# Two graph layers on one core: neighbour rows of layer 0 gathered in natural order, one closing block per 128 nodes

## What is computed

```python
h = relu(layernorm(x))
agg = segment_sum(h[src], dst, 6250)
deg = segment_sum(1, dst, 6250)
z = agg / max(deg, 1)[:, None] @ W_l.T + b_l + h @ W_r.T
r = relu(z)
x = x + (r - mean(r)) * rsqrt(var(r) + 1e-5) * gamma + beta
# layer 1: attention (Q, K, V of relu(layernorm(x))) over the same src, dst
```

## Time and profile before

| what | us |
|---|---|
| median of three runs | 3741.74 (3740.89 to 3746.67) |
| profiled execution, whole | 3740.36 |
| profiled execution, span from first to last instruction | 3738.0 |
| busy in the span: PE, DVE, POOL, ACT | 3025.4, 2503.8, 1991.4, 1632.8 |
| mean granted TensorE clock | 0.862 of full speed |

### The profile page before, as it was taken

One profiled execution on the slowest core, in us unless ns is written; L12 is line 12 of the kernel. 1 busy time (PEld: TensorE's weight loads), 2 busy tenths in 40 slices (PEclk: granted clock), 3 DMA queues, 4 the chain that ended last, 5 costly groups with the idle time before them and its releaser, 6 DMA issues. The chain is left out here.

```text
span 3738.0 us, 59649 instructions
## 1 busy us (share of the span) xinstructions
PE 3025.4 (81%) x11648; PEld 1516.3 (41%) x11649; DVE 2503.8 (67%) x4615; ACT 1632.8 (44%) x6216; POOL 1991.4 (53%) x1929
## 2 busy tenths in 40 slices
PE   4776777777777776599998999999999999999640
PEld 2332222222222222488884444444444444444210
DVE  4444333333333333555557999999999999999999
ACT  2331000000000000222226999999999999999410
POOL 1004777777777776111115555555555555555455
PEclk9887766667776767799998999999999999999865
DMA  2334666666666665344446888887888888888337
GB/s 71 110 109 133 176 176 175 177 175 180 176 175 174 176 175 153 113 143 151 147 145 245 276 277 277 278 275 270 274 276 276 276 276 277 277 276 277 104 116 218
DMA packets 263476, 750.48 MB, mean 201 GB/s; under 512 B 54179, under 2 KB 54181, under 8 KB 263402
## 3 DMA queue, kind: packets, MB, share of 16 engines
q0 software_dynamic: 197504, 615.66, 52.1%
q1 hardware_dynamic: 58910, 121.60, 10.1%
q10 hardware_dynamic: 7020, 12.80, 0.9%
HBM read 750.45 MB, written 77.83 MB: 222 GB/s over the span
## 5 line engine op out<-in xcount | busy, mean ns | idle before, releaser
L1080 POOL DMA_INDIRECT kv<-kv_d,src_t x880 | 876.9, 997 | 633.4 <-PE psw L1226 464.1
L831 POOL DMA_INDIRECT rows<-y_d,src_t x880 | 898.0, 1020 | 555.8 <-DVE rows L838 288.1
L1102 ACT ACTIVATE kv<-kv,wgt 128x64 f32<-128x64 f32 x4400 | 1096.8, 334 | 0.0
L1223 PE MATMUL psa<-kv,hot 128*128 128x512 f32 x1760 | 863.6, 613 | 29.1 <-ACT kv L1102 27.7
L921 PE MATMUL pss<-rows,hot 128*128 128x512 f16 x1760 | 632.5, 494 | 273.4 <-DMA rows<-y_d,src_t 238.0
L1132 DVE TENSOR_TENSOR kv<-kv,ps_q 128x1024 f32<-128x1024 f32 x440 | 533.0, 1211 | 32.6 <-PE ps_q L1207 24.0
L1145 DVE TENSOR_REDUCE score<-kv 128x16 f32<-128x1024 f32 x440 | 531.2, 1207 | 0.0
L1019 ACT ACTIVATE var<-var 128x512 f32<-128x512 f32 x2 | 1.3, 629 | 1187.7 <-DVE var L1006 1187.7
L1223 PEld LDWEIGHTS psa<-kv,hot 128*128 128x128 f32 x1760 | 304.1, 190 | 395.9 <-issue 387.1
L1207 PE MATMUL ps_q<-sums,hotT 128*128 x1760 | 454.4, 381 | 0.1
L855 DVE TENSOR_SCALAR rd<-psc 128x1 f32 (+1 forms) x49 | 7.7, 158 | 599.7 <-PE psc L923 599.7
(11 more groups left out here) (191 smaller groups left out, 3620.1 us busy)
## 6 DMA issues: line engine op xcount, KB each, us to landing
kv_d<-o_sb SPq DMA_DIRECT2D x49, 512.0 KB, 2.8
rows<-y_d,src_t POOLq DMA_INDIRECT x880, 3.7
kv<-kv_d,src_t POOLq DMA_INDIRECT x880, 5.3
y_d<-y SPq DMA_DIRECT2D x49, 256.0 KB, 2.0
x_d<-x_sb SPq DMA_DIRECT2D x49, 256.0 KB, 3.2
h_d<-h SPq DMA_DIRECT2D x49, 256.0 KB, 3.4
h1b<-h_d SPq DMA_DIRECT2D x49, 256.0 KB, 2.7
x1b<-x_d SPq DMA_DIRECT2D x49, 256.0 KB, 4.0
```

The costliest lines, as they stand in the source:

```text
L831: pool.indirect_dma_start(rows[:, u, g, :], None, y_d[0:N, :], bass.IndirectOffsetOnAxis(src_t[:, m:m + 1], 0), bounds_check=limit, oob_is ...
L1080: pool.indirect_dma_start(kv[:, u, g, :], None, kv_d[0:N, :], bass.IndirectOffsetOnAxis(src_t[:, m:m + 1], 0), bounds_check=limit, oob_is_ ...
L1102: last = nc.scalar.mul(v, v, wgt[:, u, g * HEADS + h:g * HEADS + h + 1])
L1223: nc.tensor.matmul(pss[:, ds(par, D)], hot[:, u, g, :].bitcast(F32), kv[:, u, g, D:2 * D], start=False, stop=(g == G - 1), skip_group_chec ...
```

## The change

1. `embed` no longer uses PE. DVE and ACT split h, not transposed, into its fp16 parts, which are stored to HBM (`h0_d`) and kept in `sums`. x has three buffers instead of two.
2. The weight preparation moves into `prepare`, between the issue of its index gathers and their use. New tables are built there, among them `nat_t`: src in natural order, 782 columns of 128, read back from `src_pad` by 7 DMAs and transposed.
3. `aggregate` gathers rows of h (the same 2 KB per row) in natural order: 391 groups, 782 gathers, no bounds check. A step finds its group's ring slot in a table; a straddling group stays in its slot for both of its steps. Rows outside a step's window are multiplied by zeros of the one-hot.
4. SP stands between: it waits for a group's landing, tells PE (`ready`), reads from a table (`last_t`) the last step that uses the group four back, waits for it and tells GpSimd (`free`).
5. PE reads four values per step in one load and takes one branch. At a new window w a block does `multiply(w-3)` (24 products: own h by W_r, average by W_l), `turn(w-2)` (8 small matmuls that transpose the fp16 parts of h, 4 transposes of the average) and the zeroing. Both of the first are behind branches of their own.
6. ACT joins aggregate: it scales the sum by 1/degree and makes the high parts. DVE makes the degree, the low parts and a shorter flush, and does so three one-hots ahead of the window's first step instead of one.
7. Eight memsets of the ring go.

The diff, cut to its core:

```diff
-    y_d = nc.dram_tensor("y_d", (WINDOWS * P, 2 * D), F16).ap()
+    h0_d = nc.dram_tensor("h0_d", (WINDOWS * P, 2 * D), F16).ap()
```

In `prepare`, DVE, behind the index columns:

```diff
+                        nc.vector.tensor_scalar(before_g[:, :], step[:, 0:GROUPS], 1.0, cnt[:, 0:1], ALU.add, ALU.is_ge).then_inc(ended, 1)
+                        for k in range(3):
+                            then(nc.vector.tensor_scalar(back_t[k][:, :], win[:, :], -(k + 1.0), 0.0, ALU.add, ALU.max))
+                            then(nc.vector.scalar_tensor_tensor(past_t[k][:, :], win[:, :], k + 1.0, new_t[:, :], ALU.is_ge, ALU.mult))
...
+                        for c in range(NCH):
+                            n = min(P, GROUPS * G - c * P)
+                            dve.wait_ge(turned, 2 * TCH + c + 1)
+                            nc.vector.tensor_copy(nat_t[:, c * P:c * P + n], ps_t[c % 2][:, 0:n]).then_inc(stored, 1)
```

In `embed`, DVE:

```diff
+                        def low(w, b):
                             dve.wait_ge(high, w + 1)
+                            nc.vector.tensor_tensor(slot(w, 1), h[:, b % 2, :], slot(w, 0), ALU.subtract).then_inc(split, 1)
```

In `aggregate`, GpSimd:

```diff
+                        for n in range(GROUPS):
+                            if n >= U:
+                                pool.wait_ge(free, n - U + 1)
                             for g in range(G):
+                                pool.indirect_dma_start(at_ring(n % U, g), None, h0_d[0:N, :],
+                                                        bass.IndirectOffsetOnAxis(nat_t[:, n * G + g:n * G + g + 1], 0)).then_inc(rows_in[n % U], 16)
```

SP:

```diff
+                        def pass_on(n, i, u, release=True):
+                            sp.wait_ge(rows_in[u], 16 * G * (i + 1))
+                            sp.sem_inc(ready, 1)
+                            if release:
+                                last = sp.value_load(last_t[0:1, ds(n - LAG, 1)], min_val=1, max_val=U + STEPS)
+                                sp.wait_ge(ps_made, last)
+                                sp.sem_inc(free, 1)
```

ACT:

```diff
+                        def high_parts(w):
+                            act.wait_ge(turned, w + 1)
+                            act.wait_ge(products, w + 1)
+                            nc.scalar.copy(mT[:, 0, :], ps_m0[:, :])
+                            nc.scalar.copy(hT[:, 0, :], ps_h0[:, :]).then_inc(high, 1)
...
+                        def average(w, par):
+                            act.wait_ge(rd_ready, w + 1)
+                            nc.scalar.mul(mean[:, :], pss[:, par * D:(par + 1) * D], rd[:, 0:1]).then_inc(averaged, 1)
```

DVE:

```diff
+                        def low_parts(w):
+                            dve.wait_ge(high, w + 1)
+                            nc.vector.tensor_tensor(mT[:, 1, :], ps_m0[:, :], mT[:, 0, :], ALU.subtract)
+                            nc.vector.tensor_tensor(hT[:, 1, :], ps_h0[:, :], hT[:, 0, :], ALU.subtract).then_inc(low, 1)
...
+                        def close_before(s):
+                            [new] = load_values(mybir.EngineType.DVE, past_t[0], s, 1, 1)
                             with dve.If(new):
...
                                 dve.wait_ge(ps_made, s + U)
                                 alone(dve)
+                                degree(w, par)
+                                [second] = load_values(mybir.EngineType.DVE, past_t[1], s, 1, 1)
+                                with dve.If(second):
+                                    low_parts(dve.value_load(back_t[1][0:1, ds(s, 1)], min_val=0, max_val=WINDOWS - 1))
+                                [third] = load_values(mybir.EngineType.DVE, past_t[2], s, 1, 1)
+                                with dve.If(third):
+                                    flush(dve.value_load(back_t[2][0:1, ds(s, 1)], min_val=0, max_val=WINDOWS - 1))
```

PE:

```diff
+                        def turn(w):
+                            pe.wait_ge(averaged, w + 3)
+                            pe.wait_ge(low, w + 1)
+                            for c in range(KC):
+                                for part in range(2):
+                                    nc.tensor.matmul(ps_h0[:, c * P:(c + 1) * P], slots[:, ds(w * 2 * WIDTH + part * D + c * P, P)], ident16[:, :],
+                                                     start=(part == 0), stop=(part == 1))
+                            for c in range(KC):
+                                last = nc.tensor.transpose(ps_m0[:, c * P:(c + 1) * P], mean[:, c * P:(c + 1) * P], ident[:, :])
+                            last.then_inc(turned, 1)
...
+                        def multiply(w):
+                            pe.wait_ge(low, w + 2)
+                            pe.wait_ge(taken, w + 1)
+                            for k, (given, weights) in enumerate(((hT, w_r16), (mT, w_l16))):
+                                for c in range(KC):
+                                    for part, of in ((0, 0), (0, 1), (1, 0)):
+                                        last = nc.tensor.matmul(ps_z[:, :], given[:, part, c * P:(c + 1) * P], weights[:, of, c, :],
+                                                                start=(k == c == part == of == 0), stop=(k == 1 and c == KC - 1 and part == 1))
+                            last.then_inc(products, 1)
...
+                                par, new, need, ring = load_values(mybir.EngineType.PE, use_t, s * 4, 4, (U - 1) * G * 2 * D)
...
+                                pe.wait_ge(ready, need)
...
+                        multiply(WINDOWS - 3)
+                        turn(WINDOWS - 2)
+                        multiply(WINDOWS - 2)
+                        turn(WINDOWS - 1)
+                        multiply(WINDOWS - 1)
```

More of the change, by code:

```diff
@@ L797, in aggregate, with windows @@
-        def aggregate(w_r16, bias, S1, S2):
+                            act.wait_ge(h_made, w + 1)
+                            nc.scalar.copy(slot(w, 0), h[:, b % 2, :]).then_inc(high, 1)
+                        def windows(q, buf, after=NB):
+                            for b in range(NB):
+                                rectify(NB * q + b, q, buf, b)
+                                if b == NB - 2:
+                                    deviation(q + 1, after)
+                        deviation(0, NB)
@@ L800, in aggregate @@
+                        for q in range(XB):
+                            windows(q, q)
+                        with act.Fori(1, FOURS // XB - 1) as i:
+                            for k in range(XB):
+                                windows(XB * i + k, k)
+                        for k in range(XB):
+                            windows(FOURS - XB + k, k, NB if k < XB - 1 else 1)
+                        rectify(WINDOWS - 1, FOURS, 0, 0)
+        def aggregate(w_l16, w_r16, bias, S1, S2):
             with ExitStack() as ctx:
-                rows = sb(ctx, "rows", [P, U, G, 2 * D], F16)
+                rows = sb(ctx, "rows", [P, U * G * 2 * D], F16)
```

485 lines of the change are left out of this document (234 added, 251 removed).

## The result

| | before | after |
|---|---|---|
| median of the runs, us | 3742.22 (3740.89 to 3746.67, 4 runs) | 4018.19 (4016.59 to 4019.79, 4 runs) |
| span of the profiled execution | 3738.0 | 4017.2 |
| first gather of aggregate starts | 316.8 | 184.0 |
| last gather starts | 1481.8 | 1708.7 |
| aggregate's last VectorE pass ends | 1490.5 | 1771.4 |

The ratio is 1.073, 95% interval 1.072 to 1.075, where 3486 us, 0.932, had been forecast. By the table: the stages before the gathers gave 132.8 us, the stretch of the gathers took 359.7 more (1524.7 instead of 1165.0), its tail 54.0 more (62.7 instead of 8.7), the rest 1.7 less; the sum is 279.2, which is the difference of the spans.

The account below looks back on a forecast made before the run. Aggregate was taken as paced by GpSimd's number of gathers. 3740.36 - 130 (embed) - 169 (gathers) + 15 (closing block) + 28 (tail) = 3484, given as 3486 us with the median's 1.4 us offset; range 3445 to 3610.

Parts of the forecast that it names:

- Embed and prepare: Stages before the gathers: weight block ends at 70 us, first gather at 187 instead of 316.8, minus 130 us.
- (d): Rival: embed's loop is held by its transfers, 12 us a quad, whole 3531 us; chance 0.10.
- Gathers: Aggregate: 782 gathers at 1.275 us replace 880 at 1.325, GpSimd setting the pace; minus 169 us (145 to 189).
- four prepared steps at 0.92: Aggregate's window chain: TensorE fills VectorE's 6.5 us with opening zeros and these steps, 4.7 us, and stalls 1.8.
- VectorE's load and branch per step fit: Aggregate: they fit into VectorE's 0.38 us gap between one-hots, part of pricing the hand-over and loads at zero.
- chain of 19.0 us per window: Aggregate, one window's last step to the next's: 1.4 us under GpSimd's 20.4 us pace; 21.6 with slow first products.
- The block: Aggregate's window closing: 24 products, 8 small matmuls, 4 transposes fit under GpSimd's pace; plus 15 us, bounds 0 and 59.
- lateness removes such stretches: Closing block: half-clock first products (1.2 us over pace per window) need prior idleness, which being late removes.
- The tail: Last gather's start to aggregate's end: 37 us instead of 8.9, plus 28 us.
- (b): Rival: aggregate is paced by bytes, not gathers; its 1166 us stays, whole 3640 us; chance 0.04.
- (a): Rival: TensorE and VectorE take turns setting aggregate's pace, 23 us per window, whole 3601 us; chance 0.20.
- (c): Rival: TensorE's clock stays at 0.50 through aggregate, 31 us per window, whole 3993 us; chance 0.03.

Follow-up runs that it names:

- e9: e5 with VectorE's aggregate loop cut from eight steps per turn to four; 3632.9 us, ratio 0.971.
- e17: e9 with natural order, TensorE looping over 391 groups at fixed places, turning before multiplying, one packed word per group for VectorE and TensorE; 3523.0 us, ratio 0.942.
- e5: Kernel after with 880 bounds-checked gathers in step order, fixed places, no SyncE hand-over, two one-value TensorE loads; 3664.0 us, ratio 0.980.
- e8: Kernel after without the closing block's 12 products of the mean with W_l; 3868.5 us, ratio 1.035.
- e13: e7 with TensorE waiting through SyncE for a count against a loaded value; 4026.0 us, ratio 1.076.
- e2: Kernel after with VectorE's aggregate loop cut from eight steps per turn to four; 4015.8 us, ratio 1.073.
- e4: Kernel before with TensorE reading its two values out of one four-value load; 3747.5 us, ratio 1.001.
- e1: Kernel after with TensorE loading one packed word per step instead of four values; 4102.1 us, ratio 1.096.
- e7: e6 with the four wide products taking the ring's place from a loaded value instead of a fixed address; 3885.5 us, ratio 1.040.
- e6: e5 with TensorE reading its values by one load of four, two of them unused; 3731.7 us, ratio 1.000.

## Why the prediction was wrong

**Embed and prepare: right.** First gather at 184.0, forecast 187. The tables' last copy ended near 70, as said, and VectorE waited for x once, 5.6 us, as the loop was entered, and a quad took 8.3 to 8.7 us. Rival (d) is out. The stage gave 132.8 us, forecast 130.

**Gathers: the duration was right, the pace was not GpSimd's.** 972 ns mean and 946 median, that of a gather without bounds check. But 566 us of waiting came on top. In e9, where nothing holds GpSimd, the pace is 1.327 a gather, and in e17 (1041 - 72 of waiting) / 781 = 1.24. The term was sound and hidden behind another bound. (Its lower end, 145, does not follow from 1.32 a gather: 1166 - 1032 is 134, which the + 35 in the range has right.)

**The step that failed: "four prepared steps at 0.92" and "VectorE's load and branch per step fit".** The chain of 19.0 us per window took TensorE's step from 848.51 to 849.43. That is the pitch of steps that the sequencer had queued while 12 products ran, here the first three behind an opening (848.51, 849.43, 850.34; the next starts at 851.86). The kernel before has two to four of them behind an opening, and else mostly waits for rows, so that the earlier trace rows and GpSimd's pace hid what a step costs the sequencer. Even that kernel's own step costs 1.6 us when nothing else holds it up: e5 has the same two loads, branch, fixed places and waits, and its "issue" steps are 1.61 apart. I priced SP's hand-over and the table loads for SP, VectorE and the opening, and for TensorE's step, which by the change "reads four values per step in one load", nothing at all. Measured: the load of four 0.988 us (0.29 a step more than two single loads), four dynamic places 0.38, the wait against a loaded value 0.29, together the way from 1.61 to 2.57; the step 2.57 in place of 0.92 for those on the chain, and in place of nothing for the rest, which the forecast had under GpSimd's 20.4. Eight of them are 20.6 us, the whole of GpSimd's window, before any block.

**The block: mis-sized.** 1.1 + 5.3 + 1.5 and 0.5 of zeros were foreseen, 8.4. Measured from the end of the step ahead (811.8) to the first product of the next (822.97) are 11.2: the gap is 1.69 and the first dozen ran at 1.2 GHz, 5.30 instead of 2.7. This block is one of the longer ones; over 45 the mean is 10.5, with a first dozen of 4.76. That is 2.1 us x 48 = 101 us, and e8 shows that nearly all of the block counts. The prediction had the slow first half in its upper bound and set it aside because "lateness removes such stretches" of idleness. It doesn't where TensorE is late because of its own sequencer: the engine then pauses in every step, and comes into the block at the low clock. With cheaper steps the first dozen's mean is 3.5 us in e5, 3.4 in e9 and, with the turning ahead of it, 2.8 in e17.

**The tail.** 62.7 us, forecast 37. The 30 us between the last step and the coefficients came as said (1740.5 to 1771.4). The other 32 are the last gather to the last step: eight groups lay in the ring, because TensorE was behind, where I had counted one.

Sum: 3486 - 3 for the start, + 513 for the stretch of the gathers (1524.7 where 1012 was forecast), + 26 for the tail is 4022; 4018 was measured.

**The rivals.** (b) is out: e17 moves 196 GB/s in this stage, above the 174 of before, so bytes did not pace it. The "small, variable" that the Trainium skill, DMA: Bandwidth & Descriptors, section "Anatomy of one DMA", gives for descriptor generation is contradicted by e9 against e17: the same bytes, 98 gathers fewer and each without the bounds check (946 ns against 998), 125 us. (a) named the right sign of trouble, GpSimd's gaps naming SP, and the wrong size, 23 us a window against 32.1; and what stood against it, that an engine that falls behind stays busy and at the high clock, did not hold: TensorE was behind and busy 72% of the time, at a mean clock of 0.67. (c) came out at 3993 and looks like a hit at 4018. It is not: its mechanism was products at 1.2 GHz in all steps, and the pitch is 2.57 at either level (826.81 and 807.30 above), so the right time was luck. The low clock came with TensorE pausing for its sequencer: from e5 to e13 only loads, addresses and a wait were added, and the granted clock from 184 to 1340 us fell from 0.87 to 0.68. Only the first dozen of a block pays for it. My chance of 0.04 for slower rested on never having asked what a step costs when nobody else holds it up.

## What to carry to other kernels

Before moving work to where an engine "has slack", price the step of each engine as if all others were free: loads by value (0.25 to 0.29 us each here, together or apart), register operations, dynamic addresses and register waits by some 0.1 to 0.3 us, and compare the sum with the pace that will be left. A pitch that stays the same while the named releaser and the clock change is a sequencer's. And an edit that is worth nothing (the short loop in e2, the four-value load in e4) may be worth 30 to 70 us once the bound above it is gone, so retry small edits after each large one.

## What the runs showed of the hardware

- A sequencer's load of four values lasts 988 ns against 287 for one: 234 for each further value and some 50 fixed.
- A register operation recorded with 32 to 46 ns takes about 0.1 us of a queue's time (an estimate from e1, eight in 0.83 us, and from e7 against e6, three in 0.38 us).
- A semaphore wait against a loaded value, with the register work of its bounds, cost 0.29 us a step more than a wait against the loop's own count (e13 against e7), also in steps that did not have to wait.
- A compare-and-branch in TensorE's queue lasted 207 ns in the median, 75 at the least (440 in the kernel after). The Trainium skill, Advanced Engine Details and Errata, section "Control Flow Timing", gives about 108 ns; the measurement decides here.
- Steps with two single loads, a branch and fixed addresses follow each other 1.61 us apart when nothing else holds them up (e5); steps that the sequencer had queued behind other work, 0.92 apart, with the same matmuls (kernel before).
- VectorE's loop of 8 steps with nested branches fetched instructions again (301 packets against 34 with 4 steps a turn), in idle stretches of up to 4.6 us. That cost 0 where TensorE was the bound (e2) and 31 us where it was not (e9).
